# One flat attention, fewer blocks and all ternary weights in the first expert loop, in a four-layer attention and FFN kernel

## What is computed

```python
# L0 FFN: 2 shared and 16 routed experts, top 4
probs = softmax(xt @ router_w.T)                      # 2048 tokens, 16 experts
topk_p, topk_i = top_k(probs, 4)                      # gates of the routed experts
y = sum over experts e of gate[:, e] * (gelu(xt @ up[e].T) @ down[e].T)
# L3 attention: bitnet layers, weights in {-1, 0, 1}, rows quantised with one scale for the tensor
qW = sign(W) * (abs(W) > 0.5 * mean(abs(W)))
i_scale = max(abs(x)) / 127;  qx = round(x / i_scale)
fused = bitnet(text, W_txt)
for Wa in (W_att0, W_att1):
    kv = bitnet(image, Wa); k = concat([kv, kv])
    fused = fused + 0.1 * softmax(fused @ k.T / 16) @ k
avg_img = mean(image over its tokens)                 # one row for each batch
h = relu(bitnet(concat([fused, broadcast(avg_img)]), W_f1))
out = bitnet(h, W_f2)
# L3 FFN: 8 experts, top 2
```

## Time and profile before

| | us |
|---|---|
| median of 3 runs | 1698.03 (1694.05 to 1701.17) |
| the profiled execution | 1712.53 |
| its span | 1710.8 |

### The profile page before, as it was taken

How to read it: one execution, slowest core, us unless ns; L and a number is a source line. 1 busy time by engine, 2 the same in 40 slices (tenths; PEclk the granted TensorE clock), 3 DMA queues, 4 the chain that set the end, 5 groups by cost and what they waited for, 6 DMA issues and landing times. The chain is left out here.

```text
span 1710.8 us, 28597 instructions
## 1 busy us (share of the span) xinstructions
PE 1438.1 (84%) x9199; PEld 1135.1 (66%) x9223; DVE 993.9 (58%) x2394; ACT 797.3 (47%) x1925; POOL 602.8 (35%) x806
## 2 busy tenths in 40 slices
PE   4689999599999999677799997784757549999995
PEld 3468888577777777444677664462534439989895
DVE  3778888855555555578666664734765434343432
ACT  2553444465555555378555652413647323333331
POOL 0156782363343333220554442900102522222222
PEclk9799999899999999989899999886988669999998
DMA  8000005049200000100000003006003821111110
GB/s 274 19 13 19 26 25 161 4 134 283 65 1 1 1 2 2 38 1 4 13 2 1 2 25 123 14 23 250 1 0 99 267 79 51 52 46 52 46 54 7
DMA packets 67340, 97.46 MB, mean 57 GB/s; under 512 B 7792, under 2 KB 56832, under 8 KB 66176
## 3 DMA queue, kind: packets, MB, share of 16 engines
q1 hardware_dynamic: 61920, 82.94, 15.8%
q0 software_dynamic: 5280, 12.74, 2.2%
HBM read 61.86 MB, written 35.63 MB: 57 GB/s over the span
## 5 line engine op out<-in xcount | busy, mean ns | idle before, releaser
L1330 POOL TENSOR_SCALAR XT<-XT,l1x_rs 128x256 f32<-128x256 f32 x256 | 117.7, 478 | 191.9 <-DVE l1x_rs L1214 191.9
L2531 PE MATMUL bank<-l3x_wd,CT 128*128 x624 | 144.8, 386 | 8.2 <-issue 7.5
L1218 DVE TENSOR_REDUCE l1x_nmax<-bank 128x2 f32<-128x512 f32 x128 | 87.4, 684 | 110.2 <-PE bank L1040 110.2
L1157 ACT ACTIVATE XT<-bank,l1x_nmax 128x256 f32<-128x256 f32 x256 | 118.8, 471 | 68.6 <-DVE l1x_nmax L1218 68.5
L2519 PEld LDWEIGHTS bank<-XT,l3x_qw 128*128 128x128 f32 x1248 | 147.9, 194 | 3.5 <-issue 0.9
L2519 PE MATMUL bank<-XT,l3x_qw 128*128 128x128 f32 x1248 | 148.4, 277 | 1.0 <-issue 0.5
L2531 PEld LDWEIGHTS bank<-l3x_wd,CT 128*128 128x128 f32 x624 | 116.5, 192 | 27.7 <-issue 12.9
L1052 PE MATMUL bank<-ident,XT 128*128 128x128 f32 x768 | 120.7, 280 | 7.5 <-DVE l2x_pt L1225 3.5
L766 DVE SCALAR_TENSOR_TENSOR X<-bank,l0f_gates,X 128x256 f32<-128x256 f32 x288 | 118.9, 473 | 1.1 <-PE bank L673 1.1
L1052 PEld LDWEIGHTS bank<-ident,XT 128*128 128x128 f32 x768 | 84.6, 140 | 41.3 <-issue 20.7
L1225 DVE COPY l1x_pt<-bank 128x512 f32<-128x512 f32 x128 | 87.8, 686 | 30.8 <-PE bank L1052 30.8
(11 more groups left out here) (529 smaller groups left out, 3892.4 us busy)
## 6 DMA issues: line engine op xcount, KB each, us to landing
slots<-blank SPq DMA_DIRECT2D x9, 1987.5 KB, 22.5
l3x_wu<-in_L_ffn_W SPq DMA_DIRECT2D x8, 1024.0 KB
l3x_wd<-in_L_ffn_W SPq DMA_DIRECT2D x8, 1024.0 KB
XT<-slots SPq DMA_DIRECT2D x39, 132.5 KB, 2.1
l0f_wu<-in_L_ffn_upT SPq DMA_DIRECT2D x18, 128.0 KB, 2.2
l0f_wd<-in_L_ffn_downT SPq DMA_DIRECT2D x18, 128.0 KB, 2.3
X<-in_x SPq DMA_DIRECT2D x1, 2048.0 KB, 8.3
l0x_later<-in_L_xattn_W_f1T SPq DMA_DIRECT2D x1, 2048.0 KB
```

The lines of the kernel that those rows point to most:

```text
L1157: act.activation(pr[n % 3][:, i, q, :], sc[(2 * n + i) % 3][:, q * S:(q + 1) * S], ACT.Exp, bias=nmax[:, n % 3, i, q:q + 1], accum_out=sum ...
L1218: dve.tensor_reduce(nmax[:, n % 3, i, :], sc[(2 * n + i) % 3][:].rearrange("p (q s) -> p q s", q=QT), AX, ALU.max, negate=True).then_inc(m ...
L1330: pool.tensor_scalar(t, t, rs[:, n % 3, i, q:q + 1], 1.0, ALU.mult, ALU.mult).then_inc(norm_ok, 1)
L2531: last = pe.matmul(y_b[i % 2][:, 0:D], hT[i % 2][:, m, :], wd[:, ds(e * HT + m, 1), :].rearrange("p a n -> p (a n)"), start=m == 0, stop=m ...
```

## The change

Three places change. The L0 FFN takes all fourteen ternary pieces, three steps an expert from expert 3 to 16, with the raw f1 and f2 loaded into the part of `K.raw` that is done with; the weights of L1's attention wait, one by one, for their part of `K.raw`. The L2 FFN loses POOL's work, the loads and the store. The router of the L0 FFN holds token rows in PE and moves its 16 columns of weights; its logits need no turning, and everything behind them comes two units (the choice one unit) earlier. In L3 the loads of kv and W1 and POOL's constants go into the layernorm's block, which now also waits for kv; the scaling of the averages goes to POOL there; the two loops of the attention become one flat list of 16 units, in which DVE also takes the maxima of the rows; and f1 reads the averages with a step of zero, so that the block that repeated them goes.

```diff
 # l0_ffn, SP
                     load(e)
+                    if e == 11:
+                        sp.wait_ge(ternary.q_ok, ternary.done(6))
+                        back.load(sp)
                 sp.wait_ge(ternary.q_ok, ternary.done(ternary.pieces()))
+                sp.dma_start(K.qweights[:, 0:ternary.columns], ternary.q[:]).then_inc(ternary.stored, 16)
                 if K.last >= 2:
-                    load_attention_weights(K, sp, "l1x")
-                ternary.store(sp)
+                    load_attention_weights(K, sp, "l1x", [(back.q_ok, back.done(n)) for n in (2, 4, 6, 0)])
+                sp.wait_ge(back.q_ok, back.done(back.pieces()))
+                back.store(sp)
+                sp.wait_ge(ternary.stored, 16)
 # l0_ffn, POOL
                     split(e)
-                    for n in range(done, min(done + 2, ternary.steps())):
-                        ternary.step(pool, n)
-                    done += 2
+                    if 3 <= e < 11:
+                        for n in range(3 * (e - 3), 3 * (e - 2)):
+                            ternary.step(pool, n)
+                    elif 11 <= e < 17:
+                        for i in range(FRONT_TERNARY, len(TERNARY)):
+                            pool.wait_ge(back.loaded[i], 16)
+                        for n in range(3 * (e - 11), 3 * (e - 10)):
+                            back.step(pool, n)
 # l0_ffn, PE
-                def route(c):
+                def route():
                     pe.wait_ge(wr_in, 16)
+                    pe.wait_ge(t_read, KD * NC)
                     pe.wait_ge(x_hi, KD * NC)
...
                     for t in range(NT):
-                        last = pe.transpose(bank[2][:, t * ER:(t + 1) * ER], lgT[:, t // TPC, t % TPC * P:(t % TPC + 1) * P], K.ident[0:ER, 0:ER])
+                        for k in range(KD):
+                            last = pe.matmul(bank[2][:, t * ER:(t + 1) * ER], XT[:, k, t * P:(t + 1) * P], wr[:, k, :], start=k == 0, stop=k == KD - 1)
                     last.then_inc(logits, 1)
...
                 outputs(1)
-                route(0)
-                route(1)
-                hidden(3)
-                outputs(2)
-                route(2)
-                route(3)
-                hidden(4)
-                outputs(3)
-                turn_logits()
-                for n in range(4, N):
+                route()
+                for n in range(2, N):
 # l0_ffn, DVE
-                    if n == 4:
+                    if n == 2:
                         logits_shifted()
+                    elif n == 4:
+                        probabilities()
                     elif n == 5:
-                        probabilities()
-                    elif n == 6:
                         choose()
 # l2_ffn
-                ternary.load(sp)
...
-                ternary.store(sp)
-
-            @block.gpsimd
-            def _(pool):
-                for i in range(FRONT_TERNARY, len(TERNARY)):
-                    pool.wait_ge(ternary.loaded[i], 16)
-                for n in range(ternary.steps()):
-                    ternary.step(pool, n)
 # shared_key_attention, DVE
+                def largest(n):
+                    b = n % B
+                    dve.wait_ge(added, n + 1)
+                    dve.tensor_reduce(maxima[:, KD * b:KD * (b + 1)], F[:, :, b * S:(b + 1) * S], AX, ALU.max, apply_absolute_value=True)
+                dve.tensor_reduce(maxima[:, KD * B:KD * B + 1], avg[:].rearrange("p k b -> p (k b)"), AX, ALU.max, apply_absolute_value=True)
+                sum_halves(0)
+                for n in range(N + 3):
+                    if n + 1 < N:
+                        sum_halves(n + 1)
+                    if n < N:
+                        maximum(n)
+                    if 1 <= n < N + 1:
+                        factors(n - 1)
+                    if 2 <= n < N + 2:
+                        copy_turned(n - 2)
+                    if n >= 3:
+                        add(n - 3)
+                    if n >= N - B + 4:
+                        largest(n - 4)
+                largest(N - 1)
 # l3_both, load (now all in the layernorm's block)
+            sp.dma_start(kv, K.kv).then_inc(kv_in, 16)
+            for e in range(E - 2):
+                sp.dma_start(wu[:, e * KD:(e + 1) * KD, :], a["L3_ffn_W1"][e].rearrange("(k p) n -> p k n", p=P)).then_inc(K.w_loaded, 16)
             sp.wait_ge(loaded, 16 * (len(ws) + 4))
+            sp.wait_ge(kv_in, 16)
...
-        with nc.Block() as block:
-            @block.vector
-            def _(dve):
-                for k in range(KD):
-                    dve.tensor_copy(qa[:, 2 + k, :].rearrange("p (b s) -> p b s", s=S), avg_q[:, k, :].unsqueeze(2).to_broadcast([P, B, S]))
-
...
-                        last = pe.matmul(bank[u % 4][:], q["f1"][:, k, m * P:(m + 1) * P], qa[:, k, c * CH:(c + 1) * CH], start=k == 0, stop=k == 3)
+                        x = qa[:, k, c * CH:(c + 1) * CH].rearrange("p (b s) -> p b s", s=S) if k < KD else avg_q[:, k - KD, 2 * c:2 * c + 2].unsqueeze(2).to_broadcast([P, 2, S])
+                        last = pe.matmul(bank[u % 4][:].rearrange("p (b s) -> p b s", s=S), q["f1"][:, k, m * P:(m + 1) * P], x, start=k == 0, stop=k == 3)
```

More of the change, by code:

```diff
@@ L191, in factors, with layernorm @@
         return self.rstd[:, ds(t, 1)], self.nmr[:, ds(t, 1)]
-def layernorm(K, name, load=None, keep=None, have_stats=False, maxima=None):
+def layernorm(K, name, load=None, keep=None, have_stats=False, maxima=None, constants=None):
     nc, X, XT, bank = K.nc, K.X, K.XT, K.bank
@@ L218, in _ @@
                     load(sp)
+            if constants:
+                @block.gpsimd
+                def _(pool):
+                    constants(pool)
             if keep is not None:
@@ L728, in _ @@
                 hidden(2)
-                copy_logits(0)
-                copy_logits(1)
-                hidden(3)
-                copy_logits(2)
-                copy_logits(3)
-                for n in range(4, N):
+                for n in range(3, N):
                     hidden(n)
-                    if n == 6:
+                    if n == 4:
                         act.wait_ge(sh, 1)
@@ L1986, in _, with shared_key_attention @@
                                        bias=bias[:, m:m + 1], scale=scale[:, j:j + 1]).then_inc(read, 1)
[L1989 removed]
+def shared_key_attention(K, name, F, kv, area, avg, maxima):
     nc, bank = K.nc, K.bank
@@ L2103, in _ @@
+                for n in range(N + 1):
+                    if n < N:
+                        exponentials(n)
+                    if n:
+                        normalise(n - 1)
+                    if n < N:
+                        copy_keys(n)
             @block.vector
@@ L2140, in _, with sum_halves @@
[L2140 to L2158 removed]
+                def sum_halves(n):
+                    b = n % B
+                    if n >= 2:
+                        dve.wait_ge(s_done, n - 1)
+                    if n >= B:
+                        dve.wait_ge(added, n - B + 1)
+                    dve.tensor_tensor(fs[:, n % 2, :], F[:, 0, b * S:(b + 1) * S], F[:, 1, b * S:(b + 1) * S], ALU.add).then_inc(fs_ok, 1)
```

242 lines of the change are left out of this document (92 added, 150 removed).

## The result

The changed kernel takes 1678.88 us, the median of 4 runs (1674.67 to 1681.90); the kernel before takes 1699.12 in the same comparison. The ratio is 0.9874, with a 95% interval of 0.985 to 0.9898: 20.2 us or 1.2% less. The forecast was 1679.5 and -18.4 us.

| stage | before | after | difference |
|---|---|---|---|
| l0_cosine | 76.1 | 74.9 | -1.2 |
| l0_ffn | 245.2 | 250.9 | +5.8 |
| l1_xattn, l1_ffn, l2_xattn | 722.4 | 721.7 | -0.7 |
| l2_ffn | 108.9 | 99.0 | -9.9 |
| l3_both | 558.2 | 532.5 | -25.7 |

A forecast was written before the change was run, and what follows sets the result against it. No single engine was taken to bound the whole: PE paces the first FFN's expert loop, other stretches are serial. Stage terms summed to -18.4 us off the 1698.03 median, forecast 1679.5 us, range 1667 to 1694.

The forecast's parts named there:

- router and choice: L0 FFN: router as 64 narrow records, -1 us (bounds -2 and +7); experts chosen two units earlier, gain 1.2 us.
- third ternary step: L0 FFN expert loop: three ternary steps an expert make POOL as full as PE; +4.5 us, bounds +1 and +14.
- its absence from the L2 FFN: L2 FFN: without POOL's ternary work DVE's chain steps run faster; -7 us, bounds -4 and -12.
- start of L3, averages' block: L3 start: loads issued earlier, kv the last wait, gain 3.5 us (bounds 0 and 7); block for the averages gone, -0.5.
- flat attention: L3 attention: two loops of 8 units become one of 16, with eight reductions added; net -2.4 us, bounds -5 and +2.
- quantisation and copies: L3 quantisation of fused rows: reductions and a memset go, -4.7 us; the block of two copies goes, -2.6.
- f1: L3 f1 product: reading averages with a step of zero changes nothing, 0 us; half rate would be +14.
- term of -6.1: L3 attention: at 3.00 us a unit, unit 15's maximum comes at 1237.1 instead of 1243.19, -6.1 us before added reductions.
- (b): L0 expert loop: POOL's combination slides over a DVE subtraction, whose wait grows until PE's period meets POOL's; 3.1 us.
- prediction's own criterion: L0 expert loop: the forecast is wrong if POOL makes PE wait more than 0.5 us an expert.
- rival 6: L0 expert loop: POOL locks DVE's subtractions out for whole instructions; +56 us instead of +4.5, total 1731; chance 0.06.
- rival of half rate: L3 f1 product: the zero-step operand halves its rate, +14 us, total 1693.5; chance 0.08.

The follow-up runs named there:

- first experiment: Changed kernel with the ternary work in its old place (two steps an expert in L0 FFN, last two weights in L2 FFN): L0 FFN 247.7 us, L2 FFN 104.8.

## Why the prediction was right, and where its steps were not

The time came out 0.6 us beside the forecast, and that is luck in good part: two steps missed by 4.7 and 5.9 us in opposite directions and cancelled, and so did smaller misses of 1.2 each. Forecast and measured by step, in us:

| step | forecast | measured | from |
|---|---|---|---|
| router and choice | -2.2 | +2.5 | first experiment, L0 FFN |
| third ternary step | +4.5 | +3.3 | first experiment, L0 FFN |
| its absence from the L2 FFN | -7 | -5.8 (-9.9 against before) | first experiment, L2 FFN |
| start of L3, averages' block | -4.0 | -2.8 | first product of the attention, 38.5 to 35.6 into the stage |
| flat attention | -2.4 | -8.3 | unit 0's maximum to DVE's end, 60.3 to 52.0 |
| quantisation and copies | -7.3 | -7.8 | from there to f1's first product, 17.4 to 9.6 |
| f1 | 0 | 0 | products of both kinds 0.22 |
| sum | -18.4 | -18.9 | medians: -20.2 |

**Router: the step that failed.** "The clock at this place before is 1.00 and PE works without a pause ahead of it, so I take 7.6." At full clock the price was right (four times 1.85). But the clock did not stay: with the 64 records of 16 columns in one run it fell, in four runs it did not. Its low half was in my bounds (+7), and I argued it away with a rule about pauses that no row had shown for narrow products. The choice of experts went as forecast and somewhat better: the mask product takes 0.43 us at its new place instead of 1.62, and PE's wait behind the choice is 2.0 us shorter, forecast 1.2.

**Attention: the other one.** The term of -6.1 was read between two maxima in mid-stream, and the rest of the attention was left as it was. In the diff, however, the copy of a unit comes ahead of the addition at the end of the pipe, where the old loop had it behind. I had listed the edit as a flattening and not followed the order of the last units. By place, the miss of 5.9 us is 2.7 behind unit 15's maximum (-0.8 measured, +1.9 forecast), most of it the new order's 2.5; 1.8 between the maxima of units 7 and 15 (-6.1 against -4.3), by a faster pace and cheaper reductions; and 1.4 ahead of unit 7's maximum, whose cause stays open. The eight reductions together cost 3.1, near the forecast's 3.7.

**Third ternary step: right in mechanism.** Forecast period 11.64 and "11.6 to 11.7 us apart with almost no idling"; measured 11.73 with none. The combination did slide over a subtraction until PE's period met POOL's, as (b) said, and PE never waited for a split. The 0.4 us that PE bears of such a wait was right too (0.41). POOL's sum was right by two errors: the splits take 3.83 us (204.41 to 208.24) and not 3.23, and both comparisons 2.84, not one of them 3.28. The size came out at 3.3 instead of 4.5. By ACT's gelus the experts 3 to 16 take 3.8 us longer than with two steps, not evenly: 0.3 in most, 1.1 and 1.2 in experts 3 and 9, where a subtraction became ready early in the combination and took 2.3 and 2.4 us, and none in experts 10 to 13; expert 2, which now has no ternary steps, is 0.8 shorter. The prediction's own criterion (POOL makes PE wait more than 0.5 us an expert) is not met: the period is 0.31 longer, through the subtraction.

**The lock, rival 6.** The page "SBUF — State Buffer" of the Trainium skill, section "SBUF: two separate sides", has it that DVE with two SBUF inputs and a POOL operation that reads SBUF hold each other off for the whole instruction. I held 0.69 us beside a comparison against it. Both are right in part: behind a combination or a split, with two SBUF inputs on POOL's side too, the subtraction waits to the end (1.55 here), as the page says; beside a comparison or the one-input step it waits through the first 0.95 us and then passes, which is less than the page says and more than I held. My one row, 2.6 us into a comparison, could not show that first part. What I priced in rival 6 was whole comparisons, so +56 us did not come.

**L2 FFN.** L1816, L1817 and L1820 fell to 0.17, 0.29 and 0.17 us, as expected. -5.8 and -9.9 are both inside the bounds of -4 to -12, and the -7 with its part for the clock lies between them. That nothing in the edited stages explained why the profiled execution of before was 14.5 us slow was not quite so: 4.1 of them may lie here.

**Start of L3.** The forecast named the right last wait, kv, and let it land 6.6 us after qw (1163.9 to 1170.5); it takes 7.9. The error is in the rate: 5 us for 2 MB is about 400 GB/s, which the engines did not hold between the small loads and at kv's end. The first reduction so gains 1.8 us and not 3.5; the rest of the 2.8 lies in the block for the averages and around it.

**f1.** The rival of half rate is refuted by the rows above.

## What to carry to other kernels

A sum can be right because its errors cancel; only step-by-step runs, read stage by stage, tell which price to trust next time. When a loop is rewritten, compare the order of the steps at both ends of its pipe and not only in the middle. A run of narrow products was dearer than the same products between wide ones, and an engine that is filled up to the pace of the critical one sets the pace through every lock that it holds, not only through its sum.

## What was unexpected in the hardware

- PE's granted clock fell from 1.00 to 0.50 in a stretch in which PE's records had no gap (9.15 us), in nine of nine kernels with 64 records of 16 columns in a row. With four runs of 16 records between products of 512 columns it stayed.
- A POOL instruction of 1024 bf16 columns with two SBUF inputs (2.14 us) holds a DVE subtraction with two SBUF inputs until it ends (1.55 and 1.78 us instead of 0.69, up to 2.42); one with a single SBUF input on as many columns (2.77 us, and comparisons of 2.84) holds it only through about its first 0.95 us.
- The wait turns into a period: 11.29 us an expert without it, 11.42, 11.73 and 11.97 with a subtraction of 1.24, 1.55 and 1.78 us in each.
- In the profiled execution of the changed kernel a stretch of unchanged code took 83.5 us, and 91.4 to 94.4 in the eleven other kernels, each of which has a wait of 12 to 14 us there that the changed kernel's has not. Two single profiles can differ by 10 us in code that nobody touched.
